# Turning the gated rows ahead of the diagonal product in a Mamba and mixture block

## The reference

```python
proj = einsum('bsd,ed->bse', x, in_proj_w)           # gate | hBC | dt
hBC = silu(conv4(hBC) + conv_b)                      # hs, Bm, Cm
xch = hs * dt
Y_diag = einsum('bzlhn,bzshn,bhzls,bzshp->bzlhp', Cc, Bc, L, xch)
states = einsum('bzlhn,bhzl,bzlhp->bzhpn', Bc, decay_states, xch)
Y_off = einsum('bzlhn,bzhpn,bhzl->bzlhp', Cc, prev, exp(A_cum))
g = (Y_diag + Y_off + hs * D) * silu(gate)
out = rms_norm_per_group(g) * norm_w
return einsum('bsi,oi->bso', out, out_proj_w)
```

## Time and profile before

| | us |
|---|---|
| median of 3 runs | 1628.3 |
| lowest, highest | 1627.63, 1630.69 |
| the profiled execution | 1630.77 |
| its span, first to last instruction | 1629.5 |
| PE busy (matmuls) | 1601.3 |
| VectorE busy | 1385.6 |
| GpSimd busy | 1333.7 |
| ACT busy | 1244.2 |

### The profile page before, as it was taken

The page is one execution under the profiler, slowest core; times in us unless marked ns, Lnnn a source line. Parts: engine busy times, 40 slices in busy tenths (PEclk is TensorE's granted clock), DMA queues, the critical chain, the costliest instruction groups (busy, mean ns, idle before and its releaser), DMA issues.

```text
span 1629.5 us, 31884 instructions
## 1 busy us (share of the span) xinstructions
PE 1601.3 (98%) x10792; PEld 1301.9 (80%) x10792; DVE 1385.6 (85%) x1678; ACT 1244.2 (76%) x2628; POOL 1333.7 (82%) x1238
## 2 busy tenths in 40 slices
PE   7989999999999999999999999999999999999999
PEld 5777888878888888888888888888888878888777
DVE  5868789897888879898898978988798988989788
ACT  5267787877878878787877879788787878778774
POOL 3147689996899979898799968999788987999796
PEclk9999999999999999999999999999999999999999
DMA  4153265544655455445654456545564455544453
GB/s 128 56 201 115 98 181 166 175 134 122 183 147 149 142 157 163 117 137 147 188 153 129 129 142 175 160 130 153 148 163 122 130 165 159 171 122 140 131 162 105
DMA packets 216402, 236.13 MB, mean 145 GB/s; under 512 B 154280, under 2 KB 155824, under 8 KB 212016
## 3 DMA queue, kind: packets, MB, share of 16 engines
q1 hardware_dynamic: 216240, 234.08, 49.8%
HBM read 147.52 MB, written 55.05 MB: 124 GB/s over the span
## 4 chain that ended last, share of the span: by engine, by line
PE 85%; POOL 5%; DVE 4%; issue 2%; ACT 2%; DMA 1%; SPq 0%; DVEq 0%; ACTq 0%; POOLq 0%
PE P L265 9%; PE P L267 9%; PE P L266 9%; PE P L502 7%; PE P L359 6%; PE P L342 6%; PE P L343 6%; PE P L349 6%; PE P L360 6%; PE P L366 6%; PE P L374 4%; PE P L490 1%; PE P L487 1%; PE P L481 1%; PE P L479 1%
## 5 line engine op out<-in xcount | busy, mean ns | idle before, releaser
L606 ACT ACTIVATE P<-AB,SC 128x128 f32<-128x128 f32 x1016 | 307.4, 362 | 20.3 <-DVE EM L950 20.1
L265 PE MATMUL P<-xh,AH 128*128 128x512 f32 x656 | 261.9, 399 | 2.4 <-DVE xl L981 1.9
L267 PE MATMUL P<-xh,AL 128*128 128x512 f32 x656 | 255.9, 390 | 0.0
L266 PE MATMUL P<-xl,AH 128*128 128x512 f32 x656 | 255.5, 389 | 0.0
L833 DVE SCALAR_TENSOR_TENSOR hsX<-P,cwt,hsX 128x1023 f32<-128x1023 f32 x189 | 241.8, 1279 | 13.4 <-ACT hsX L543 8.9
L342 PE MATMUL P<-GH,xh 128*128 128x512 f32 x512 | 212.5, 415 | 0.0
L359 PE MATMUL P<-OH,gTh 128*128 128x512 f32 x508 | 199.7, 393 | 4.5 <-DVE Gt L926 2.3
L343 PE MATMUL P<-GH,xl 128*128 128x512 f32 x512 | 201.4, 393 | 0.0
L360 PE MATMUL P<-OH,gTl 128*128 128x512 f32 x508 | 197.9, 390 | 0.0
L1164 POOL TENSOR_TENSOR AL<-AR,AH 128x512 fp32r<-128x512 f32 x82 | 108.8, 1327 | 81.3 <-ACT AH L530 81.3
L950 DVE TENSOR_TENSOR EM<-P,Gt 128x1024 f32<-128x1024 f32 x127 | 154.7, 1218 | 21.6 <-issue 21.0
(11 more groups left out here) (231 smaller groups left out, 4172.8 us busy)
## 6 DMA issues: line engine op xcount, KB each, us to landing
AB<-acr_d SPq DMA_DIRECT2D x128, 512.0 KB, 4.6
half_d<-hsX SPq DMA_DIRECT2D x60, 512.0 KB, 3.6
AR<-in_wa SPq DMA_DIRECT2D x80, 256.0 KB, 2.7
TS<-in_wg SPq DMA_DIRECT2D x16, 1024.0 KB, 5.1
TS<-in_wo SPq DMA_DIRECT2D x16, 1024.0 KB, 6.9
part_d<-pl SPq DMA_DIRECT2D x64, 256.0 KB, 3.3
pl<-part_d SPq DMA_DIRECT2D x64, 256.0 KB, 3.6
SC<-sct_d SPq DMA_DIRECT2D x16, 128.0 KB, 5.2
```

Source lines behind the costliest of these rows:

```text
L265: te.matmul(o, ah_, bh_, start=(first and i == 0), stop=False)
L266: te.matmul(o, ah_, bl_, start=False, stop=False)
L267: r = te.matmul(o, al_, bh_, start=False, stop=(last and i == n - 1))
L606: r = se.activation(decays(m)[:, h, :], AB[m % 2][:, h, :], ACT.Relu, bias=SC[s % 2][:, c, 3, h:h + 1], scale=-1.0)
```

## The change

R(m-1) moves in slots 1 to 126 from behind Y(m) to the place between O(m-2) and Y(m), in TensorE's program and in the table of banks. Slot 127 had that order already. No other engine's program changes. Banks and semaphore counts stay the same.

```diff
             jobs += [("O", m - 2, (4,))] if m >= 2 else []
-            jobs += [("GTr", m - 1, (5,))] if m == M - 1 else []
+            jobs += [("GTr", m - 1, (5,))] if m else []
             jobs += [("Y", m, (7,))]
-            jobs += [("GTr", m - 1, (5,))] if 0 < m < M - 1 else []
             jobs += [("GT", m + 1, (6,))] if m + 1 < M else []
...
                 if m >= 2:
                     pe_output(m - 2)
-                if m == M - 1:
+                if m:
                     pe_turn_gated(m - 1)
                 banks_free("Y", m)
...
                 r.then_inc(s_y, 1)
-                if 0 < m < M - 1:
-                    pe_turn_gated(m - 1)
                 if m + 1 < M:
                     pe_gate(m + 1)
```

## The result

The changed kernel took 1633.84 us (median of 8 runs, 1632.68 to 1634.35), the kernel before 1628.97 us in the 8 runs beside it (1627.63 to 1632.69). The ratio is 1.0022, with a 95% interval of 1.0012 to 1.0031: slower by 4.9 us. The forecast was 1634.1.

What follows compares the result with a forecast made beforehand. TensorE's own instruction stream was taken to bound 113 of 128 slots. 117 slots at 0.055 us gave +6.4, shorter Gt waits at most -0.6, together +5.8 on the median 1628.3: 1634.1 us, range 1629 to 1638.

Steps and rivals of the forecast that it cites:

- What bounds the kernel: Slots 3 to 115: TensorE's own instruction stream sets the time, busy 1354.71 of 1357 us; in slots 122 to 125 VectorE.
- The gain of the earlier turn, 0: ACT gets the turned rows about 1.4 us earlier, but O does not wait for them; gain costed at 0.
- The stream, 0.055 a slot over 117 slots, 6.4 us: TensorE, first L366 load to G's third load: 3.03 us before, 3.09 after; 0.055 longer in 117 slots, 6.4 us.
- all four pieces: TensorE load distances after the change: L366 to R 0.92, R to Y 0.75, Y to G 1.08, G to third 0.34.
- the unknown one: Y straight to G, which no slot showed at the high clock: 1.08 us between first loads.
- The waits, -0.6: TensorE's 12 weight-load waits for Gt each shrink by 0.055 us, at most 0.6 us in all.
- new waits of L359 for Gt: Sign of a larger loss: O's loads waiting for Gt after slots 35, 51 and their like; 1637.3 us, chance 0.07.
- The sum, +5.8: Whole kernel: 6.4 us of stream less at most 0.6 of Gt waits, +5.8 us on the median 1628.3.
- Y's 0.45 us later, 0: Y ends 0.45 us later in the slot for VectorE, which adds to it at L906; cost taken as 0.
- the 1.96 us of idle time in slot 35: VectorE's 1.96 us stand for the tanh of the gate, claimed to swallow Y's 0.45 us delay.
- The rival of no change: TensorE's tile-size switches stay two a slot at one price, or the gap behind Y vanishes: 1627 us, chance 0.13.
- Faster: TensorE's exit from Y scales with the clock, stretch 2.92 us, 0.115 less a slot: -13 us, 1615, chance 0.05.

Runs made afterwards that it cites:

- experiments 2 and 3: 2: new order in even or odd strips only, 1.0031 and 1.0020; 3: changed kernel, ACT's gTh copy waits for Y, 1.0031; ratios to kernel before.
- split_3_1: Kernel before with three of the four turns R ahead of Y, the fourth behind it: 1628.94 us, ratio 1.0008 to the kernel before.
- late_copy: Changed kernel, but ACT copies gTh only when Y is done: 1632.99 us, ratio 1.0031 to the kernel before.

## Why the prediction was right, point by point

- **What bounds the kernel** held. Most of the loss is TensorE's stream (4.4 us of 6.1 in the traces), and no relief of another engine shortened it.
- **The gain of the earlier turn, 0**, is right on TensorE's path. But "what it does next is the tanh of the gate product" was only half of what ACT does: ahead of the tanh stands AH, for which GpSimd waits. The step costed the relief by what it could give, not by what it sets going.
- **The stream, 0.055 a slot over 117 slots, 6.4 us**: all four pieces were right to 0.01 us, and so was the unknown one, built from slot 49, slot 127 and slot 0. The term was mis-sized by where the stretch ended. It is 0.033 and 0.040 a slot, 4.4 us in all. When TensorE comes out of the turns or of Y, the first wide pair is spread out (312 or 337 ns) and several of the starts behind it are slow too, in the new order fewer of them than in the old one; a stretch must be measured to where both run at their usual 227 ns.
- **The waits, -0.6**: wrong in sign. They came to +1.7 in the traces. The seven of slots 16, 32, ... went, and seven longer ones came in the slots ahead of them, by a mechanism that the text did not have. The text said that "new waits of L359 for Gt" would prove it wrong, in slots 35, 51 and their like; they came there too, but only at 0.06 to 0.16 us.
- **The sum, +5.8** against +4.9 by medians and +6.1 by the traces without chance waits: 2.0 too much in the stream, 2.3 too little in the waits. That the sum came out so near is luck, since the two errors cancel; that the change costs a few microseconds of TensorE's stream is not.
- **Y's 0.45 us later, 0**: right within 0.7 us. L903 waits 20 times for Y, not 9, and slots 122 to 125 take 36.71 us from slot 122's first matmul of Y to that of slot 126, 36.76 before. But the 1.96 us of idle time in slot 35 was the wrong cover to read. What counts is how long Gt is ready before O, which was 0.50 us in that slot. In slots 35, 51 and 67 Gt starts 8.0 us behind the first matmul of Y in both kernels, so the delay reached it in full (in slot 51 half of it by a longer dxh, 1.55 us for 1.31), and some 0.4 us of the 0.5 went. That goes with the 0.6 to 0.7 us of waits in slots 19, 35, 51 and their like; experiments 2 and 3, with 0.5 to 0.8 us in each of them, show how little cover is left.
- **The rival of no change**, with the rule of the Trainium skill, "TensorEngine Tiling (Array Packing)", Key Properties, that every change of tiling mode drains TensorE: the changes are as many in both kernels, two a slot, as the trace shows, but they are not one price. Leaving wide matmuls costs 318 ns for Y and 231 for R; G behind Y costs 152, behind R 28. The rule gives no price. If each change had the same one, split_3_1, with the same number of them as both, would be as slow as either, and its slot is 6 to 7 ns shorter than the one's and 40 to 47 shorter than the other's.
- **Faster** (the exit scaling with the clock): 152 ns from Y to G here, 245 in slot 0 at half the granted clock. That is a factor of 1.6, not 2.

## What to carry over

When engines take turns on a full TensorE, price a new order by the starts of its pieces, and run the stretch on until both orders are back at their steady pace. A relief that is "worth nothing" on an idle engine still moves that engine's later work against its neighbours: follow it one engine further, to the results that the full engine waits for. Put such results ahead of an instruction whose duration depends on the neighbour, and keep one narrow matmul between small tiles and a wide group.

## What the hardware showed that I had not expected

- After f32 matmuls (turns, Y) the wide fp32r matmuls of G do not run at 227 ns a matmul at once. The starts in an odd strip before: 312, 229, 234, 235, 225, 230, 236, 229, 232, 231, 227. After: 338, 236, 228, 233, 230, 227, 227, 226, 227, 227, 226. The longer first distance is followed by fewer slow ones. In even strips of the changed kernel they last longer (337, 231, 230, 236, 229, 232, 231, 227). The same row stands behind O's wait for Gt in slot 48 of the kernel before (335, 229, 234, 235, 225, 230, 236), where no f32 matmul is near, so it may belong to any break in the stream. What decides the number stays open.
- How long VectorE's dxh (128x512 f32) takes is set by what GpSimd is doing at its start. The fourteen traces of this case have it 1568 times. In 78 cases GpSimd is idle when it starts, and it takes 0.68 to 0.69 us, even in the 14 of them in which GpSimd starts an instruction 0.05 us later; there it is GpSimd's xch that lasts longer, 1.55 us where it mostly has 1.05. In the other 1490 a GpSimd instruction is running. In 1322 of these dxh ends 0.54 to 0.565 us after that instruction does, however long that is (0.87 and 1.78 us in slot 47, 0.82 in late_copy); all but 2 of the rest start in its last 0.15 us. So it is the order of the starts that decides, and not how much of the two overlaps.
